# Expert attention: where on SyncE's queue the next batch's spread queries and keys are loaded

## The reference

```python
def expert_step(acc, params):
    q = (x @ qw.T + qb_).reshape(B, S, H, Dh).transpose(0, 2, 1, 3)
    k = (x @ kw.T + kb_).reshape(B, S, H, Dh).transpose(0, 2, 1, 3)
    v = (x @ vw.T + vb_).reshape(B, S, H, Dh).transpose(0, 2, 1, 3)
    scores = jnp.einsum('bhqd,bhkd->bhqk', q, k) * scale
    p = jax.nn.softmax(scores, axis=-1)
    o = jnp.einsum('bhqk,bhkd->bhqd', p, v)
    o = o.transpose(0, 2, 1, 3).reshape(B, S, E) @ ow.T + ob_
    return (acc + o * g[..., None], None)
```

## Time and profile before

| | |
|---|---|
| median of 3 runs | 2467.38 us (2462.93 to 2471.3) |
| profiled execution: span of the records | 2469.5 us, 52904 instructions |
| expert stage within it, from the first weight load to the last rows DMA | 161 to 1222 us |
| PE busy, share of the span | 1995.8 us (81%) |
| DVE | 1761.0 us (71%) |
| ACT | 1453.6 us (59%) |
| POOL | 1028.3 us (42%) |
| DMA | 77.07 MB, on average 31 GB/s |

### The profile page before, as it was taken

How to read it: one execution, slowest core, us unless ns; L and a number is a source line. 1 busy time by engine, 2 the same in 40 slices (tenths; PEclk the granted TensorE clock), 3 DMA queues, 4 the chain that set the end, 5 groups by cost and what they waited for, 6 DMA issues and landing times. The chain is left out here.

```text
span 2469.5 us, 52904 instructions
## 1 busy us (share of the span) xinstructions
PE 1995.8 (81%) x18992; PEld 926.7 (38%) x18992; DVE 1761.0 (71%) x3039; ACT 1453.6 (59%) x2138; POOL 1028.3 (42%) x1009
## 2 busy tenths in 40 slices
PE   5647888888888888888847988988988988888886
PEld 3421222222222222222223554654554554555454
DVE  4736666676666666666658978878878877887794
ACT  4313556666555656555726766756757657666573
POOL 0011111111111111111039968858758767686680
PEclk9856889999899999888969998999999999999998
DMA  1022222222222222222010000000000000000000
GB/s 32 2 52 51 45 54 55 47 51 49 44 52 56 52 56 52 56 52 54 2 58 1 2 29 10 12 30 10 12 31 10 12 30 10 12 30 11 12 2 10
DMA packets 52105, 77.07 MB, mean 31 GB/s; under 512 B 10899, under 2 KB 45749, under 8 KB 48053
## 3 DMA queue, kind: packets, MB, share of 16 engines
q1 hardware_dynamic: 51317, 74.06, 13.0%
q10 hardware_dynamic: 576, 0.15, 0.0%
HBM read 47.70 MB, written 25.69 MB: 30 GB/s over the span
## 5 line engine op out<-in xcount | busy, mean ns | idle before, releaser
L902 DVE TENSOR_REDUCE ENM<-PM 128x1 f32<-128x512 f32 x1024 | 656.5, 685 | 335.9 <-PE PM L735 328.4
L832 ACT ACTIVATE EPT<-PA 128x1024 f32<-128x1024 f32 x512 | 520.0, 1021 | 212.0 <-PE PA L747 199.9
L735 PE MATMUL PM<-EKX,EQX 48*128 48x512 bf16 x1024 | 359.7, 414 | 177.0 <-DMA EKX<-e_park 91.0
L1216 POOL TENSOR_TENSOR DRN<-DRN,DHALF 128x8 f32<-128x8 f32 x192 | 364.5, 1899 | 7.4
L655 POOL CAST ENMP<-ENM 128x16 bf16<-128x16 f32 x64 | 12.6, 196 | 847.8 <-DVE ENM L902 847.8
L1214 POOL TENSOR_TENSOR DQR<-DR 128x512 f32<-128x512 f32 x192 | 244.2, 1272 | 246.9 <-DVE DR L1497 245.5
L735 PEld LDWEIGHTS PM<-EKX,EQX 48*128 48x128 bf16 x1024 | 83.6, 95 | 585.4 <-DVE ENM L902 404.1
L757 PE MATMUL PV<-EPT,EVP 128*32 128x512 f32 x2048 | 295.2, 651 | 0.9 <-ACT EPT L832 0.7
L747 PE MATMUL PA<-EQX,EKX 51*128 51x512 bf16 x1024 | 263.2, 404 | 5.2 <-DMA EQX<-EROWS 4.9
L1259 PE MATMUL PM<-DWQKV,DXS 128*128 128x512 f32 x384 | 216.6, 647 | 39.5 <-ACT XNT L1456 23.2
L1495 DVE TENSOR_TENSOR DR<-DRAW,DTAB 128x512 f32<-128x512 f32 x192 | 193.1, 1005 | 61.9 <-POOL DQR L1219 28.2
(11 more groups left out here) (204 smaller groups left out, 2930.8 us busy)
## 6 DMA issues: line engine op xcount, KB each, us to landing
e_park<-EPARTS SPq DMA_DIRECT2D x64, 192.0 KB, 2.9
EQX<-e_park SPq DMA_DIRECT2D x32, 384.0 KB, 5.6
EKX<-e_park SPq DMA_DIRECT2D x32, 384.0 KB, 9.2
DWQKV<-in_WqkvR SPq DMA_DIRECT2D x6, 1536.0 KB, 6.3
e_park<-EPARTS SPq DMA_DIRECT2D x64, 128.0 KB, 2.6
e_park<-EPARTS SPq DMA_DIRECT2D x64, 64.0 KB, 2.1
EQX<-EROWS SPq DMA_DIRECT2D x256, 3.0 KB
DWO<-in_WoR SPq DMA_DIRECT2D x6, 512.0 KB, 4.3
```

Source lines behind the costliest of these rows:

```text
L735: pe.matmul(PM[:, r, :], lhsT=QX[64 * r:64 * r + KQ, b, hp, t * 128:(t + 1) * 128], rhs=KX[64 * r:64 * r + KQ, b, hp, :], start=True, stop ...
L832: s_.activation(PT[:, kt, pair * 2 * S:(pair + 1) * 2 * S], PA[:, 2 * pair:2 * pair + 2, :].rearrange("p a b -> p (a b)"), ACT.Exp, scale= ...
L902: v.tensor_reduce(NM[:, g % 2, t, j, 0:1], PM[:, r, :], AX.X, ALU.max, negate=True).then_inc(maxed, 1)
L1216: g.tensor_tensor(rn, rn, HALF[:, 0:8], ALU.pow).then_inc(rooted.sem, 1)
```

## The change

In the first slot of a pair `bring_in` is called right behind `take_out` (at g = 0 behind `load_qk`), instead of in the second slot behind `rows`. No instruction is added or taken away. The wait of `bring_in` for the parked parts moves with it, and so do its four DMAs: they now stand ahead of the four DMAs of `rows` of the second slot.

```diff
                         take_out(eb, gb // HG)
                         if g == 0 and not last:
                             load_qk(e + 1)
-                    if "v" in uses:
-                        eb, gb = ahead(e, g, HG)
                         bring_in(eb, gb // HG)
                     if g == 2 and not last:
                         sp.wait_ge(filled, use(e, 1, "v"))
```

## The result

| | before | after |
|---|---|---|
| median of 20 runs | 2467.43 us | 2473.94 us |
| lowest to highest | 2455.96 to 2475.41 | 2467.36 to 2478.35 |
| profiled span | 2469.5 us | 2470.4 us |
| mean granted clock of the execution (1 is 2.4 GHz) | 0.908 | 0.895 |
| PE idle at the 15 stalls, sum | 71.9 us | 59.4 us |

The ratio of after to before is 1.0026, 95% interval 1.0016 to 1.0035: slower by 4 to 9 us, where 12 us less were forecast. The mean clocks are medians over 21 executions of before and 20 of after, so the lower one after is no chance of the one that was profiled. The other rows of the table are each read from one profiled execution, and these two differ by 0.9 us only where the medians differ by 6.5.

What follows compares the result with a forecast made beforehand. PE's 15 waits for spread keys (71.9 us), plus slow-clock work behind them, bounded what the change could reach. 8 × 1.1 + 7 × 0.5 = 12.3 us off 2469.5 gives 2457.2, less 2.1 is 2455; forecast 2446 to 2462, range 2436 to 2482.

Steps and rivals of the forecast that it cites:

- The load and the rows: Spread load on SP starts 5.0 or 4.3 us earlier; PE's stall moves to the rows at step 0; gain 12.3 us.
- 0.1 was taken from EOW: Rows DMAs behind the spread load on SP's queue land 0.1 us after it, as the 64 KB EOW load did.
- the bounds of −0.5 and 0.9: Rows landing from 0.5 us ahead of the spread load to 0.9 behind it: gains of 21 us and 0 us.
- The slow clock I leave equal: Behind PE's stalls, time from resuming to the full clock is taken as before, with no term in the sum.
- the 2 us that the prediction itself named as a sign of being wrong: PE's stalls: prediction wrong if the time at half clock changes by more than 2 us per stall.
- rival 3: Behind the stall, half clock takes in 3.7 us more work: 36 us slower, about 2503; half of it 2479; chance 0.17.
- the prediction's 0.46: Slot after the stall: 1.9 us lost in 4.1 us at half clock, 0.46 for each us.
- The period of two pairs: Sign in the profile after, expert stage: the period of two pairs shrinks by 1.6 us.
- Rival 1: Rows DMAs slip past the load on SP's queue, stall gone: 110 to 130 us less, about 2347; chance 0.05.
- Rival 2: Shorter PE stalls keep the full clock in some pairs: in all eight 32 us more gain, about 2423; chance 0.08.
- Rival 4: Rows land 0.9 us or more behind the load, the gain of 12 is gone: 2462 to 2472; chance 0.15.

Runs made afterwards that it cites:

- Experiment 4: Kernel before, with the load in two halves: queries right behind the parking, keys behind the rows as before; 2369.57 us.
- experiment 10: Kernel after, with the four rows DMAs of the second slot issued by ACT on its own queue; 2488.53 us.
- Experiments 2 and 3: Useless matmuls on PE ahead of its wait: five at step 0 in the kernel after, 2424.54 us; seven in step 2 in the kernel before, 2436.87 us.
- 1, wait at step 0: Kernel before, with PE waiting for the spread loads already ahead of step 0 of the third slot; 2528.51 us.
- 5, g = 4 only: Kernel before, with the load moved at g = 4 alone (7 pairs without weight loads); 2470.69 us.
- 6, g = 0 only: Kernel before, with the load moved at g = 0 alone (7 pairs with weight loads, one without); 2476.54 us.
- 8 and 9: Kernel after, with useless matmuls behind PE's restart: three dense float32 over 128 rows, 2489.36 us; ten thin bf16 over 48 rows, 2542.14 us.
- 7, split, weights behind: Kernel with the load in two halves, and the next expert's query and key weights loaded behind the keys in the second slot; 2354.53 us.

## Why the prediction was wrong

**The load and the rows: right.** The load starts where the forecast put it (1.5 us behind the parking, and at the end of the weight loads), takes 11.8 and 12.1 us where 12.0 were taken, and the stall moves from the spread keys to the rows. The eight stalls without weight loads last 3.4 us on average (forecast 3.6), the seven others 4.6 (forecast 5.2). The forecast's stalls make a sum of idle time that is 8 × 1.2 + 7 × 0.5 = 13.1 us less; it was 12.5. Experiment 4 shows the cause: with half the bytes ahead of the rows they are nearly in time; experiment 10 corrects its wording. PE goes on 0.6 to 0.7 us behind the last spread landing (317.44 against 316.8, 382.50 against 381.8) where 0.1 was taken from EOW; the bounds of −0.5 and 0.9 held it.

**"The slow clock I leave equal": the step that failed.** It was put in as an assumption, on the ground that each stall of before dropped the clock. That it also comes back as soon after the restart was not argued: a term put at nothing. It comes back 3.1 us later, 46.5 us in all, and with what is slow within the stalls the half clock grew by 54.6 us, 3.6 per stall, past the 2 us that the prediction itself named as a sign of being wrong. Experiments 2 and 3 show that this is what ate the gain: with the clock kept up, the moved load is ahead by 12 us. Experiments 1, 5 and 6 show that the place of the restart is enough to lengthen the slow stretch, and 8 and 9 that the kind of work behind it can shorten it to 5.0 us or stretch it to 16.2.

Which part of the work behind step 0 does it in the kernel after is argued, not shown. Before, PE restarts in step 2 and turns the maxima 4.3 us later, with float32 matmuls over 128 rows (324.39); after, the steps 0 and 1 come first and the turn starts 9.1 us behind the restart (391.64). But float32 matmuls over 128 rows into 32 columns (`mix`, the PV rows) stand close behind the restart in both kernels, and PE waits 0.35 us for maxima twice after where it waited once before. The turn doesn't end the slow stretch by itself either: in the pair of the earlier trace rows the clock came back 5.8 us behind it. That the slow stretch would take in more work was rival 3, with 0.17.

**Its price, put together.** In the seven kernels without useless matmuls and with all issues on SP, PE stands and runs slow for different times. With the idle sum as it is, two numbers fit their medians within 3.5 us: time = 2350 + idle + 0.35 × (slow us behind restarts).

| | idle us | slow us | by the formula | measured |
|---|---|---|---|---|
| before | 71.9 | 139.5 | 2471 | 2467.4 |
| after | 59.4 | 186 | 2474 | 2473.9 |
| 1, wait at step 0 | 118.3 | 169.5 | 2528 | 2528.5 |
| 5, g = 4 only | 62.8 | 163.5 | 2470 | 2470.7 |
| 6, g = 0 only | 69.4 | 163.5 | 2477 | 2476.5 |
| 4, split | 5.8 | 42 | 2371 | 2369.6 |
| 7, split, weights behind | 3.0 | 0 | 2353 | 2354.5 |

(Slow us are 15 times the mean from restart to full clock, from one execution each.) For the change: −12.5 + 0.35 × 46.5 = +3.8 us, against the 4 to 9 us measured. That is the direction, but a sum of this size is no larger than the misfit of the formula. The 0.35 rests on the two split kernels. Between the others, in which all 15 stalls drop the clock, the prediction's 0.46 does better: against before it gives +8.9, +1.9, +8.5 and +60 us for the change and experiments 5, 6 and 1, where +6.5, +2.2, +8.0 and +62 were measured. For the split ones it promises 14 and 19 us too much, so a slow us removed to the last is worth less than one moved, and why isn't shown. Rival 3 itself, at full size, let the 3.7 us grow to 6.9 and lost 48 us by it; the stretch grew by 3.1 us, which is 16 to 21 us.

**The others.** The time of 2474 lies outside the forecast of 2446 to 2462. The period of two pairs, which was to shrink by 1.6 us, shrank by 0.2 (first stall to fifteenth: 904.2 us before, 902.8 after). Rival 1 fell: the rows never slip past, not even on ACT's queue. Rival 2 fell: a stall of 2.69 us dropped the clock like the rest. Rival 4 was half true (0.6 where it needed 0.9) and decided nothing.

**Still open.** What it is in the dense matmuls that brings the clock back isn't told apart: data type, rows, or both; nor what the 0.35 us gaps add to a slow stretch. Nor why the stretches have only the few lengths given above, which puts the long ones now in one kind of pair and now in the other. And no experiment separates what ACT's issues cost.

## What to carry to other kernels

A large load moved ahead of a small urgent one can make the small one late, and another queue did not help here; load in parts, and put each part where its own deadline allows. The same idle time of PE can cost more in another place, because the half clock behind it lasts as long as the work that follows lets it, so a moved stall must be costed with the work behind its new place. Where a stall drops the clock again and again, removing it is worth more than its length (here 69 us less idle time made 114).

## What the runs showed of the hardware

- A PE that works almost without a gap can stay at 1.2 GHz for 14 to 20 us: behind the restart ten bf16 matmuls of 48 rows (5.7 us without a gap, with the steps' own) and the attention steps, with two waits of 0.35 us, left it there, and three float32 matmuls over 128 rows brought 2.4 GHz back within 3.5 to 6.3 us, 15 times of 15 (experiments 8 and 9).
- 12 KB in four DMAs on ACT's queue, issued from 307.83 to 310.66 beside 1.5 MB on SP's whose last issue began at 307.9, moved no packet before 313.8 and let PE go 0.5 us after the landing of the load (experiment 10).
